# Self-attention's row-sum reciprocal: Ln and Exp on ScalarE in place of VectorE's RECIPROCAL

## The reference, cut to what matters

```
x = x + attn(layernorm(x))            # x is 4 x 128 x 512: B=4, T=128, C=512; 16 heads of 32
q, k, v = x @ Wq.T, x @ Wk.T, x @ Wv.T        # per head
att = softmax(where(j > i, -inf, q @ k.T / sqrt(32)))
out = (att @ v) @ Wo.T
```

## Time and profile before

| | |
|---|---|
| median of 3 runs | 970.15 us |
| the profiled execution | 964.08 us |
| its span on the core | 962.3 us |
| PE busy | 695.7 us (72%) |
| DVE busy | 434.7 us (45%) |
| ACT busy | 245.8 us (26%) |
| POOL busy | 255.9 us (27%) |
| mean granted TensorE clock | 0.837 of full speed |
| self-attention's four rounds | from 660 to 707 us of the span |

### The profile page before, as it was taken

How to read it: one execution, slowest core, us unless ns; L and a number is a source line. 1 busy time by engine, 2 the same in 40 slices (tenths; PEclk the granted TensorE clock), 3 DMA queues, 4 the chain that set the end, 5 groups by cost and what they waited for, 6 DMA issues and landing times.

```text
span 962.3 us, 9595 instructions
## 1 busy us (share of the span) xinstructions
PE 695.7 (72%) x3580; PEld 322.4 (33%) x3580; DVE 434.7 (45%) x1279; ACT 245.8 (26%) x464; POOL 255.9 (27%) x213
## 2 busy tenths in 40 slices
PE   3745256386271345889679999998773599999997
PEld 1312122242140233334234444444433233333333
DVE  2405799769678785057730013403945311111113
ACT  0442546554755441200002100013501011111110
POOL 2699058657747724000000000000002100000003
PEclk9765567597595587999879999998976799999999
DMA  9721103041033051930000040300045479999954
GB/s 303 287 73 48 40 0 131 22 159 38 22 131 132 22 175 55 369 143 1 0 0 1 0 175 0 142 33 1 2 174 215 157 284 375 360 374 375 374 214 145
DMA packets 63520, 133.67 MB, mean 139 GB/s; under 512 B 8112, under 2 KB 18160, under 8 KB 62960
## 3 DMA queue, kind: packets, MB, share of 16 engines
q1 hardware_dynamic: 59536, 124.46, 35.8%
q0 software_dynamic: 1920, 6.29, 2.2%
q10 hardware_dynamic: 2016, 2.30, 0.7%
HBM read 122.62 MB, written 8.32 MB: 136 GB/s over the span
## 4 chain that ended last, share of the span: by engine, by line
PE 53%; DVE 23%; POOL 9%; ACT 6%; issue 4%; DMA 2%; SPq 1%; DVEq 1%; ACTq 0%; POOLq 0%
PE PS L1225 6%; PE PS L1361 6%; PE PS L1231 6%; PE PS L1379 5%; PE PS L1192 5%; PE PS L1123 4%; PE PS L1060 4%; DVE KA L786 3%; PE PS L1248 3%; PE PS L1366 3%; PE PS L1385 3%; DVE KA L796 2%; DVE AR L824 2%; POOL AR L429 2%; DVE V L795 2%
## 5 line engine op out<-in xcount | busy, mean ns | idle before, releaser
L404 POOL TENSOR_TENSOR RS<-VE,CST 128x1 f32<-128x1 f32 x16 | 9.4, 587 | 345.8 <-DVE VE L748 345.8
L1101 PE MATMUL PS<-AR,QT 32*128 32x512 f32 x128 | 45.2, 792 | 64.8 <-ACT AR L568 64.8
L786 DVE MAX8 KA<-AR 128x8 f32<-128x64 f32 x512 | 66.4, 208 | 39.4 <-POOL AR L488 39.0
L1060 PE MATMUL PS<-CST,TT 128*128 128x128 f32 x64 | 15.1, 418 | 85.7 <-ACT AR L594 46.1
L1085 PE MATMUL PS<-AR,WK 128*128 128x512 f32 x96 | 56.6, 752 | 23.7 <-DVE EV L843 12.9
L1029 DVE COPY AR<-PS 128x512 f32<-128x512 f32 x10 | 6.8, 691 | 138.5 <-PE PS L1060 138.5
L1192 PE MATMUL PS<-AR,TT 128*128 128x512 f32 x128 | 59.7, 623 | 2.2 <-ACT TT L654 2.2
L535 POOL DMA_INDIRECT AR<-expert_rows,SLU x8 | 8.4, 1048 | 194.6 <-DMA expert_rows<-TT 192.4
L1225 PE MATMUL PS<-TT,AR 128*128 128x512 f32 x128 | 57.9, 616 | 0.7 <-issue 0.7
L1379 PE MATMUL PS<-AR,TT 128*32 128x512 f32 x512 | 56.4, 592 | 0.8 <-issue 0.8
L1361 PE MATMUL PS<-AR 128*32 128x512 f32 x512 | 56.6, 594 | 0.0
(11 more groups left out here) (273 smaller groups left out, 1302.9 us busy)
## 6 DMA issues: line engine op xcount, KB each, us to landing
AR<-in_w SPq DMA_DIRECT2D x32, 2048.0 KB, 12.2
AR<-in_ctxT SPq DMA_DIRECT2D x16, 768.0 KB, 4.5
AR<-in_ctx SPq DMA_DIRECT2D x16, 768.0 KB, 7.4
AR<-in_W SPq DMA_DIRECT2D x2, 4096.0 KB, 20.2
token_rows<-AR SPq DMA_DIRECT2D x1, 2560.0 KB, 14.8
AR<-token_rows SPq DMA_DIRECT2D x5, 512.0 KB, 5.9
X<-in_x SPq DMA_DIRECT2D x2, 1024.0 KB, 5.3
AR<-AR POOLq DMA_DIRECT2D x8, 256.0 KB, 3.6
```

Source lines behind the costliest of these rows:

```text
L786: last = eng.max(CAND[0][:, n, :], s[:, n * G // NCH:(n + 1) * G // NCH])
L1060: return eng.transpose(dst, src, c("ident", rows)[:, 0:rows])
L1101: mm(PS[:, 2 * (k % 2) + j, :], QT[r, t], KT[b % 2][r, cols], start=True, stop=False)
```

## The change

DVE's reciprocal goes. ACT computes the same number as exp(−ln(sum)): Ln from bank 7 into `ARC`, then Exp in place with scale −1, which counts a new semaphore, `a_rec`. DVE's product waits for `a_rec` in place of `av_ps`. The pair of activations of round u stands in ACT's program behind the exponentials of round u+1 and ahead of the copies of round u+1; the last pair stands at the end.

```diff
+            def row_reciprocals(u):
+
+                eng.wait_ge(S_["av_ps"], u + 1)
+                if u:
+                    eng.wait_ge(S_["ao_sb"], u)
+                link(eng.activation(ARC, PS[:, 7, :], ACT.Ln))
+                eng.activation(ARC, ARC, ACT.Exp, scale=-1.0).then_inc(S_["a_rec"], 1)
+
             for u in range(4):
                 for j in range(4):
                     n = 4 * u + j
                     eng.wait_ge(S_["a_shift"], n + 1)
                     eng.activation(PB[:, j, :], PB[:, j, :], ACT.Exp, scale=SCALE).then_inc(S_["a_exp"], 1)
+                if u:
+                    row_reciprocals(u - 1)
                 for j in range(4):
...
                     eng.activation(PBT[:, j, :], PS[:, 4 + j % 2, :], ACT.Copy).then_inc(S_["pt_sb"], 1)
+            row_reciprocals(3)
...
-                eng.wait_ge(S_["av_ps"], u + 1)
-                link(eng.reciprocal(ARC, PS[:, 7, :]))
+                eng.wait_ge(S_["a_rec"], u + 1)
                 tt(TT[:, u, :], PS[:, 6, :], ARC, mul).then_inc(S_["ao_sb"], 1)
```

## The result

The changed kernel is slower: 972.89 us in the median of 10 runs, against 968.5 for 10 runs of before. The ratio is 1.0045 (95% interval 1.0031 to 1.0058), or +4.4 us: small, but clear of the noise. Two later groups of runs gave 1.0033 (1.0017 to 1.0049) and 1.0040 (1.0020 to 1.0060). The forecast was +4.7 us, or 974.8 us, counted from a median of 3 runs of before (970.15). With 10 runs that median is 968.5, and most of the 1.9 us between 974.8 and 972.89 is this.

A forecast was written before the change was run, and what follows sets the result against it. DVE was taken to bound the self-attention rounds at 9.41 us each. Values of round 3 at +5.5 us, less 0.8 in the tail, gave +4.7, so 974.8 us for the median (before: 970.15); range 972.2 to 978.4.

The forecast's parts named there:

- DVE bounds the rounds, and what it waits for sets them: Self-attention rounds: DVE is what a round costs, 9.41 us from product to product, with no idle time.
- The pair costs 3.85 us: ACT, from the round's last exponential to ARC: two loads of 1.28, Ln 0.60, Exp 0.63; DVE's reciprocal took 3.35.
- Products of rounds 0 to 2: DVE's products in self-attention: later than before by 0.83, 2.06 and 3.28 us, with a period of 10.63.
- The low clock in the values of round 2: PE's values of round 2 end near 698.6 with the low clock; Ln can't start before 699.4, so the delay is hidden.
- Values of round 3: PE in self-attention: they wait for ACT's last held-back copy and start at 704.97 against 699.46, +5.5 us.
- The tail of 2.58 us: Round 3, from row sums to product: 2.58 us where the reciprocal took 3.39, so 0.8 comes back.
- The sum, +4.7: Last product of self-attention at 711.3 against 706.63, moving the kernel's end by as much: +4.7 us.
- rival 4: PE's clock stays at half for longer in the output projection: 1.8 us more, +6.5, 976.6 us; chance 0.06.
- Rival 1: One table serves Ln and Exp, or loads cost next to nothing: −4.3 us, 965.9 us; chance 0.04.
- rival 3: PE's clock comes back earlier: full at the projection's start 973.0 us, also for values of round 3 971.1; chance 0.07.
- Rival 2: On ACT, a load waits until the full activation ahead has left the engine: +9.1, 979.2 us; chance 0.04.

The follow-up runs named there:

- loads_only: Kernel before, DVE's reciprocals kept, with two useless table loads ahead of the copies of rounds 1 to 3: 972.8 against 969.75 us, ratio 1.0022.
- last_on_act: Kernel before with DVE's reciprocals in rounds 0 to 2 and ScalarE's Ln and Exp for round 3 alone: 962.79 us, ratio 0.9973.
- the control: Kernel before, unchanged, run in the first group: 964.69 against 964.7 us, ratio 1.000.
- behind_copies: Changed kernel with the Ln and Exp pair of each round moved behind the next round's copies: 980.1 us, ratio to before 1.0151.
- one_set: Changed kernel with one table set holding Ln and Exp, loaded by name once ahead of the stage: 957.16 us, ratio to before 0.9914.
- one_set_inner: Changed kernel with one table set for Ln and Exp, and the pair ahead of the next round's last exponential: 960.35 us, ratio to before 0.9888; again 960.29, 0.9904.

## Why the prediction was right

- *DVE bounds the rounds, and what it waits for sets them.* Right. Against before, the change without its loads gave −7.5 us, no reciprocal −12, and the pair moved later +15.4.
- *The pair costs 3.85 us.* It took 3.83 (686.34 to 690.17), and 3.84 with the 0.01 ahead of the first load. Ln was 0.597 us in all four cases, the forecast 0.60; the Exp 0.63; each load 1.28, with 0.01 to 0.02 us on either side. So no load drains the engine, behind an Ln of full width either.
- *Products of rounds 0 to 2 at 680.73, 691.37 and 702.0.* They came, with 1.18 added, at 680.73, 691.39 and 702.04. The low clock in the values of round 2 stayed hidden, as forecast: they ended at 696.26, and their Ln started at 698.29.
- *Values of round 3 at 704.97, bound by the last copy.* Right in kind, 0.4 us too early: 704.18 + 1.18 = 705.36. The term that was mis-sized is the 2.92 us for the copies, taken over from before. From the first copy's start to the last one's end it was 3.30 (700.73 to 704.03), for the third copy waited 0.78 us for its transposes. Those took 1.94 us, where they had taken 1.56 (before, then after):

```profile
696.71 1.56 PE L1060 MATMUL PS<-CST,AR 128*128 128x128 f32 x8 [2.56 <-ACT AR L680]
```

```profile
701.46 1.94 PE L1070 MATMUL PS<-CST,AR 128*128 128x128 f32 x8 [4.18 <-ACT AR L690]
```

 PE's clock had been falling in that place before (full in 693 to 696, half from 699) and was now down all the way through. loads_only, with copies just as late, has the same 0.78.
- *The tail of 2.58 us.* 2.64 (707.88 to 710.52), against 3.39 before: the 0.8 us came back. last_on_act shows the same 0.8 by itself.
- *The sum, +4.7.* The stage gave +5.1 and the medians +4.4, +3.9 and +4.3 by group. So something outside the stage made up for about 1 us, and that the total came nearer to the forecast than the stage did is luck in part: its reasons I had not named. The clock is not it. It cost 0.8 to 0.9 us in the projection (rival 4 below), but the matmuls behind it, those of the experts' gate, gave about as much back (before, then after):

```profile
727.75 4.96 PE L1317 MATMUL PS<-GWT,TT 128*128 128x16 f32 x24
```

```profile
732.50 4.15 PE L1327 MATMUL PS<-GWT,TT 128*128 128x16 f32 x24
```

 From the stage's first matmul to PE's first instruction behind the gate it is 75.7 to 75.8 us in the three profiles of before and 80.95 to 80.97 in those of the changed kernel, so +5.1 to +5.3 still. What is seen lies ahead of the stage. In the cross-attention, which the change doesn't touch, the kernel before has an instruction of VectorE that takes 2.20 us in place of 0.22 (or, in the profile of before, a group of four copies that takes 2.85 in place of 0.67). First the control, then the changed kernel:

```profile
166.07 2.20 DVE L801 SCALAR_TENSOR_TENSOR FL<-C,V 128x1 f32<-128x1 f32 x1
```

```profile
166.09 0.22 DVE L812 SCALAR_TENSOR_TENSOR FL<-C,V 128x1 f32<-128x1 f32 x1
```

 All three profiles of the changed kernel lack this stall, all three of the kernel before have it, and the attention begins at 658.8 to 659.3 in the one and at 660.2 to 661.9 in the other. What makes it was not settled, nor whether it is in every run of a kernel. last_on_act lacks it too, and begins at 659.85; behind_copies, with the changed kernel's instructions in another order, has it, and so have one_set and one_set_inner, whose gains are then not from this.
- *Rival 1, one table.* It did not happen of itself: the kernel as changed loads twice a pair. Asked for in one_set, it has the place and sign that I gave it. Its size was under-estimated, −4.3 against −7.5, mostly since the clock stood still in my working. In one_set it is granted in full when the projection starts (rival 3's mechanism, which I had as a matter of chance). Why it is there isn't shown: in one_set_inner, whose rounds are shorter still, it falls to half just there.
 The Trainium skill ("ScalarE: Activation LUTs", section "Table sets: the hidden batching unit") says that Ln and Exp together need one load from natural_log_exp_and_others. By the changed kernel's rows that isn't so of itself, with two loads to a pair; with that set loaded by name the trace agrees with it.
- *Rival 2, a drain,* falls, and with it for this kernel the 1380 ns of drain that the Trainium skill has ("ScalarE: Activation LUTs", section "What ACT_TABLE_LOAD costs"): what the trace shows is 0.01 us (689.53 to 689.54) behind the load and 0.01 to 0.02 ahead.
- *Rivals 3 and 4, the clock.* The projection's 24 matmuls took 13.16 us against 12.29, 0.9 more. The mean of 0.58 in 714 to 717 is half clock for 84% of it, so the full clock came at 716.5, 5.3 us after the projection's start, against 3.6 before. The two later profiles of each have 12.93 and 12.94 against 12.13. So rival 4 was there with half of its price up to the end of those matmuls, and the gate's matmuls, 0.8 shorter, paid it back. Rival 3 was not there.

## What to carry to other kernels

Work moved to an idle engine costs as much as before if the engine that gave it up waits for it, and more if the new engine has to switch its function table: compare the chain on the new engine with the instruction removed, not the busy times. Two functions that alternate on ScalarE should come from one table set, loaded by name; here that alone turned +4 us into −7.5. Then look at the place of the moved work in the new engine's program: it should stand ahead of what the waiting engine does not need, and what is queued behind it (here the copies) is late by as much as it takes.

## What the runs showed of the hardware beyond that

- PE had gaps of 0.8 us and shorter ones in the last expert pair, in every profile of two groups of runs and in none of another, for all kernels alike. The 64 matmuls took 8.5 to 9.8 us with them and 3.66 without. The kernel before took 964.7 us in the group without and 969.4 to 969.75 in the two with them. What makes them was not settled.
- A stall of 2 us in short VectorE instructions came and went with the program (2.20 us against 0.22 in one of them), 500 us ahead of the code that differed. A change of 0.2% in the total needs the stage in the profile beside it.
- The clock moves a gain both ways: in one_set the projection took 10.57 us, in one_set_inner, whose rounds are shorter, 12.26 and 12.26 again in its second profile. What one stage loses by it the next can give back: 4.21 us for the gate's 24 matmuls in one_set_inner, 5.04 in one_set.
